# Waiting for each indirect scatter of token rows, and V rows of 160 halves: attention and mixture-of-experts layer on one core

## What is computed

```python
x = x + attention(layernorm(x))            # causal softmax attention, 16 heads
xf = layernorm(x)
shared = (silu(xf @ sg.T) * (xf @ su.T)) @ sd.T
probs = softmax(xf @ gate_w.T); topw, topi = top_k(probs, 2)
topw = topw / (topw.sum(-1, keepdims=True) + 1e-20)
routed = sum over experts e of ffn_e(xf) * (weight that token gives e, or 0)
return x + shared + routed
```

## Time and profile before

| | us |
|---|---|
| median of 3 runs | 918.35 |
| the runs | 915.56 to 918.37 |
| the profiled execution, its own time | 914.5 |
| its span in the trace | 912.8 |

### The profile page before, as it was taken

The page is one execution under the profiler, slowest core; times in us unless marked ns, Lnnn a source line. Parts: engine busy times, 40 slices in busy tenths (PEclk is TensorE's granted clock), DMA queues, the critical chain, the costliest instruction groups (busy, mean ns, idle before and its releaser), DMA issues.

```text
span 912.8 us, 25700 instructions
## 1 busy us (share of the span) xinstructions
PE 851.0 (93%) x10266; PEld 576.5 (63%) x10266; DVE 692.0 (76%) x1769; ACT 685.1 (75%) x843; POOL 714.1 (78%) x450
## 2 busy tenths in 40 slices
PE   5888999999999999999999999999999888959996
PEld 3445666666666666666666666666666564438885
DVE  6898888797979897979797979787976465434444
ACT  5466888988888889798989898888899782224442
POOL 3566898998999899899989898989889877244442
PEclk9799999999999999999999999999999999779999
DMA  6030232324242323333302020202020001112214
GB/s 185 21 110 10 56 68 65 68 56 70 63 79 61 69 74 68 71 63 79 60 5 55 5 48 1 58 2 49 2 49 2 2 2 47 42 35 69 62 44 146
DMA packets 60149, 48.33 MB, mean 53 GB/s; under 512 B 8688, under 2 KB 57714, under 8 KB 59904
## 3 DMA queue, kind: packets, MB, share of 16 engines
q1 hardware_dynamic: 57760, 42.48, 20.3%
q0 software_dynamic: 2272, 4.22, 1.3%
HBM read 13.93 MB, written 16.29 MB: 33 GB/s over the span
## 4 chain that ended last, share of the span: by engine, by line
PE 59%; DVE 24%; POOL 4%; issue 4%; DMA 3%; ACT 3%; another core or an unknown queue 2%; SPq 1%; POOLq 0%; DVEq 0%; ACTq 0%
DVE row_max L1034 10%; PE st L1312 7%; PE st L1313 7%; PE bg L1237 7%; PE pv L1344 5%; PE pv L1346 5%; PE pv L1348 4%; POOL p_parts L589 4%; DVE junk L1030 3%; PE bg L1487 3%; PE bg L1227 3%; PE bg L1204 2%; PE bg L1202 2%; PE bg L1203 2%
## 5 line engine op out<-in xcount | busy, mean ns | idle before, releaser
L589 POOL TENSOR_TENSOR p_parts<-prob,p_parts 128x1024 f16<-128x1024 f32 x320 | 612.4, 1936 | 89.9 <-ACT p_parts L724 87.9
L723 ACT ACTIVATE prob<-st,p_bias 128x1024 f32<-128x1024 f32 x320 | 331.1, 1035 | 109.8 <-PE st L1313 70.8
L724 ACT ACTIVATE p_parts<-st,p_bias 128x1024 f16<-128x1024 f32 x320 | 330.8, 1034 | 0.0
L1034 DVE TENSOR_REDUCE row_max<-bg 128x1 f32<-128x512 f32 x384 | 250.4, 684 | 6.9 <-PE bg L1237 5.4
L1344 PE MATMUL pv<-v_parts,p_parts 128*128 128x65 f16 x2176 | 233.0, 193 | 3.1 <-POOL p_parts L589 2.6
L1346 PE MATMUL pv<-v_parts,p_parts 128*128 128x64 f16 x2176 | 233.3, 195 | 0.0
L1348 PE MATMUL pv<-v_parts,p_parts 128*128 128x65 f16 x2176 | 232.2, 192 | 0.0
L1312 PE MATMUL st<-qk_parts 128*128 128x512 f16 (+3 forms) x640 | 221.2, 348 | 4.7 <-ACT p_parts L724 1.9
L1344 PEld LDWEIGHTS pv<-v_parts,p_parts 128*128 128x128 f16 x2176 | 202.5, 96 | 28.4 <-DVE attn L1086 8.8
L1313 PE MATMUL st<-qk_parts 66*128 66x512 f16 (+3 forms) x640 | 220.1, 350 | 0.0
L1237 PE MATMUL bg<-qk_parts 128*128 128x512 f16 (+3 forms) x640 | 210.7, 352 | 9.8 <-DVE row_max L1034 2.2
(11 more groups left out here) (231 smaller groups left out, 1044.9 us busy)
## 6 DMA issues: line engine op xcount, KB each, us to landing
qk_parts<-qk_parts SPq DMA_DIRECT2D x192, 64.0 KB, 2.0
row_dram<-fill SPq DMA_DIRECT2D x8, 1290.0 KB, 10.0
qk_parts<-qk_parts SPq DMA_DIRECT2D x16, 256.0 KB, 3.0
stage_raw<-ffn_w SPq DMA_DIRECT2D x16, 176.0 KB, 2.6
v_parts<-row_dram SPq DMA_DIRECT2D x39, 64.5 KB
qk_parts<-y_dram SPq DMA_DIRECT2D x8, 256.0 KB, 4.3
w_raw<-qkv_w SPq DMA_DIRECT2D x8, 192.0 KB, 2.3
down_w<-ffn_w SPq DMA_DIRECT2D x1, 1536.0 KB, 8.0
```

The source lines that it names most:

```text
L589: nc.gpsimd.tensor_tensor(o, a, b, ALU.subtract).then_inc(p_lo_ready, 1)
L723: nc.scalar.activation(o32, src, ACT.Exp, bias=p_bias[:], scale=D ** -0.5)
L724: nc.scalar.activation(o16, src, ACT.Exp, bias=p_bias[:], scale=D ** -0.5).then_inc(exp_done, 1)
L1034: nc.vector.tensor_reduce(row_max[:, t, c:c + 1], bank, AX_X, ALU.max).then_inc(bg_drained, 1)
```

## The change

Two edits. In `scatter_rows`, each indirect DMA of a half except its first now waits until `x_scattered[g]` has reached 16 for every scatter of that half issued before it. In the layout of V, a row has 160 halves in place of 129; the high part and the ones keep columns 0 to 64, and the low part moves from column 65 to column 96.

```diff
-VW = 2 * D + 1
+V_LO = 96
+VW = 160
...
                     for t in range(8 * g, 8 * g + 8):
+                        sent = 8 * r + t - 8 * g
+                        wait(pool, x_scattered[g], 16 * sent)
                         nc.gpsimd.indirect_dma_start(
...
-                    nc.vector.tensor_tensor(v_quad(i % 2, q, D + 1, VW), quad, v_quad(i % 2, q, 0, D), ALU.subtract
+                    nc.vector.tensor_tensor(v_quad(i % 2, q, V_LO, V_LO + D), quad, v_quad(i % 2, q, 0, D), ALU.subtract
...
-                    nc.tensor.matmul(out[:, 0:D], p_hi[:, n % PRING, cols], v[:, D + 1:VW],
+                    nc.tensor.matmul(out[:, 0:D], p_hi[:, n % PRING, cols], v[:, V_LO:V_LO + D],
```

## The result

| | before | after |
|---|---|---|
| median, 4 runs each, on one chip | 916.95 us | 944.11 us |
| all runs | 914.94 to 918.37 | 942.08 to 947.1 |
| the profiled execution, its own time | 914.5 | 942.08 |
| its span | 912.8 | 940.3 |

The ratio of after to before is 1.030, with a 95% interval of 1.0261 to 1.034: the changed kernel is slower by 27.2 us (24 to 31). The forecast was +24.5 us and 942.9.

What follows compares the result with a forecast made beforehand. The prediction took PE as the bound, with tile 9 made late by POOL's waiting scatters: +22.5 us delay, +2.0 clock and 0 for V's rows gave +24.5 on the 918.35 median, 942.9 us, range 932 to 951.

Steps and rivals of the forecast that it cites:

- The period: POOL's row scatters: start to landing 2.2 us plus release to start 0.8 us, 3.0 us for each waiting scatter.
- The train's end: Half 1's last row scatter on POOL starts at 845.7 us and SP goes on at 848.0.
- SP and PE behind it: SP's gather of tile 9 after the train: PE turns the tile at 850.8 instead of 828.24, +22.5 us.
- What the delay covers: Before tile 9: tile 0's 3.8 us lateness and ACT's two waits cost nothing within 24 us of PE slack.
- The result scatters: POOL's 39 result scatters queued behind the train: reached at 847.0 us, no cost.
- The clock: PE after its idle time, from 850.8 us: lower granted clock costs +2.0 us, between 0 and +4.
- V's rows: PE's V matmuls with 160-half rows: 0 us; rival that they matter in part, -8 us, 935 us, chance 0.07.
- The stretches of the earlier trace: ACT's unexplained waits near the trains, 6.48 and 9.56 us: worth nothing in the change unless one falls after 850.
- overlap: Rival: POOL prepares a scatter beneath the earlier landing; period 2.2 us, not slower, 918 us; chance 0.06.
- shorter period: Rival: POOL's scatter period about 2.4 to 2.6 us, 15 us less, 928 us; chance 0.07.
- late stall: Rival: an ACT stall falls after 850 us, +6.5 to +9.6 us, 949 to 952 us; chance 0.07.

Runs made afterwards that it cites:

- one wait a half: Ninth scatter of each half waits for the first eight, with V's rows of 160, against the kernel before: 904.58 us, ratio 0.9877.
- two in flight: Each scatter waits for the one two ahead, with V's rows of 160, against the kernel before: 899.73 us, ratio 1.0043.
- the two comparisons: V's rows of 160 halves alone, scatters unchanged, against the kernel before on two chips: 913.27 us, ratio 0.9983, and 913.51 us, ratio 0.9975.
- third group: The changed kernel, and one wait in each half with V as before, against the kernel before at 913.89 us: 945.57 and 904.36 us.
- three in flight: Each scatter waits for the one three ahead, V as before, against the kernel before at 895.12 us: 894.86 us, ratio 0.9996.

## Why the prediction was right, point by point

**The period: right in kind, 5% short.** Predicted 3.0 us, measured 3.145 and 3.17. From landing to start it was 0.78 to 0.80 (predicted 0.8) at 28 of the 30 waits and 0.85 at two, although POOL had nothing else to do but prepare. From start to landing it was 2.27 to 2.57, in the mean 2.37 (predicted 2.2): this is the mis-sized term. I had two ends of it in hand, 2.3 from SP's waits and 2.11 from a lone scatter of results, and took a value between them; the rows of the very same instruction said 2.3, and were the better ones, though still 0.07 short. Worth 15 x 0.145 + 15 x 0.17 = +4.7 us.

**The train's end.** Predicted 848.0 for SP, measured 850.97 (the chain above): +4.7 for the period, -1.8 since the train began at 752.68 and not at 754.44. That start is not a clean measure of anything: with the same V rows other traces have from 752.96 (one wait a half) to 757.11 (two in flight).

**SP and PE behind it: right.** From SP's release to the turn 853.65 - 850.97 = 2.68 us, predicted 2.74. The gather landed 1.80 us after its start, not 2.0.

**What the delay covers: right.** PE was ready for tile 9 at 853.65 - 28.61 = 825.0. Predicted was 826.6, by a slip: the text says three more tiles, the sum has 4 x 2.1; three at the named pace, 13.8 / 6 = 2.3, give 804.4 + 6.9 + 13.8 = 825.1. The slip changed nothing, since PE was idle behind either. Tile 0 at 804.97 (predicted 804.4) cost nothing. The 25.4 us can be followed through: half 1 has landed 850.96 - 812.4 = 38.6 us later, of which 10.2 by its later start (801.13 against 790.96) and the rest by its 15 waits. From that go the 8.9 us in which the landed train had waited for DVE's table, and 5.1 us of lead that the gather had: before, 828.24 - 821.28 = 6.96 us lay between its issue and the turn, now 853.65 - 851.75 = 1.90. To it come the 0.8 that SP takes from its release to the gather, which before lay within the 8.9: 38.6 - 8.9 - 5.1 + 0.8 = 25.4.

**The result scatters: right.** Six went out from 849.94 to 856.60, the first five 1.28 us apart, and PE never waited for gathered rows behind tile 9. SP did wait for result scatters, 7.2 us in seven waits ahead of its gathers from 850 on, against 11.3 in nine in before from 828 on.

**The clock: right.** Windows of after: length, busy time (count) of PE, PEld, ACT, DVE and POOL, granted clock, DMA share, GB/s, to be read as the earlier trace rows.

```profile
830.00:849.00 19.00, 0.00 (x0) 0.00 (x0) 0.00 (x0) 0.00 (x0) 6.17 (x7) 0.50 0.07 21
852.00:855.00 3.00, 1.35 (x6) 1.33 (x7) 0.29 (x1) 0.27 (x1) 2.14 (x3) 0.50 0.32 91
855.00:858.00 3.00, 3.00 (x15) 2.15 (x14) 0.50 (x2) 0.46 (x1) 1.95 (x2) 0.53 0.31 88
858.00:862.00 4.00, 4.00 (x32) 3.23 (x31) 1.91 (x6) 1.77 (x6) 0.97 (x1) 1.00 0.21 57
```

The first row is the changed kernel in one line: for 19 us no engine but POOL does anything, and POOL a third of the time. The clock is at 1.2 GHz until about 858 and at 2.4 from then on. Beyond tile 9's 25.4 us the span grew by 27.5 - 25.4 = 2.1 us; predicted 2.0. Nearly all of it lies in one step: from tile 9 to tile 10 857.69 - 853.65 = 4.04 us passed, where before had 830.36 - 828.24 = 2.12.

**V's rows: wrong, by a little.** I took 0, with -8 us as a rival. The groups of the three V matmuls by form, first with 129 halves (the kernel with the waits alone), then with 160 (after): busy us, mean ns of one, idle time before.

```profile
L1346 PE MATMUL pv<-v_parts,p_parts 128*128 128x65 f16 x2176 | 233.0, 193 | 3.1 <-POOL p_parts L589 2.6
...
L1348 PE MATMUL pv<-v_parts,p_parts 128*128 128x64 f16 x2176 | 233.3, 195 | 0.0
...
L1350 PE MATMUL pv<-v_parts,p_parts 128*128 128x65 f16 x2176 | 232.2, 192 | 0.0
```

```profile
L1347 PE MATMUL pv<-v_parts,p_parts 128*128 128x65 f16 x2176 | 230.3, 194 | 3.1 <-POOL p_parts L590 2.6
...
L1349 PE MATMUL pv<-v_parts,p_parts 128*128 128x64 f16 x2176 | 230.2, 193 | 0.0
...
L1351 PE MATMUL pv<-v_parts,p_parts 128*128 128x65 f16 x2176 | 230.2, 193 | 0.0
```

PE is busy for 698.5 us with them at 129 halves and 690.7 at 160, 7.8 us less. The eight traces with V rows of 129 halves have 231.8 to 233.5 us a line, the six with 160 have 230.2 to 231.3. Of these 7.8 us 1.4 and 2.5 reached the time in the two comparisons, and only the second excludes none. The step that failed is the comparison of two sets in the earlier trace rows: both sets are rows of 129 halves, so it could show only a cost that one has and the other does not, and 7.8 us / 544 = 0.014 us a set is barely more than the 0.01 us in which the rows are written. It was a fair argument against 23 us, and none against 8. Whether it is the pitch of 160 or the low part's place at column 96 that helps was not tried, nor why most of the gain in PE's busy time does not arrive.

**The stretches of the earlier trace rows: right in the sum, not understood.** I said that in the changed kernel they are worth nothing, gone or not, and that holds: PE has 28.6 us to spare there. But I had not seen what they are worth in the kernel before: on the third group's chip, where it takes 913.89 us, a single pause in each train wins 9.5 us. For a prediction of this change that did not matter; for a better kernel it is the larger finding.

**The rivals.** The *overlap* fell: from landing to start 0.78 us or more passed each time; so did the *shorter period*. The Trainium skill, DMA: Bandwidth & Descriptors, "Anatomy of one DMA", gives an estimate of 2.15 us for such a DMA; the trace has 2.29 and 2.56 us from start to landing in the rows above, 0.14 and 0.41 more, and 3.15 for the whole step, so here it comes near the transfer alone and is not the period. The *late stall* did not come: none of the three traces with every scatter waiting has a "remote" wait of ACT or DVE from 750 to 850 us, nor has after one of ACT up to 930. *V's rows* were worth some 2 us, not 8.

**Against which time.** I added 24.5 to the first median of before, 918.35; the runs beside those of after put it at 916.95, so that 1.4 us of my 942.9 come from the base. The change itself was 2.7 us larger than I said; in the profiled executions it was 27.5 us, 3.0 larger, of which 2.9 are the period and the earlier start together (4.7 - 1.8). In the third group it was larger still, 31.7 us.

## What stays open

- What the stall is. It was in all four traces that I read of kernels with unbroken trains on the chips where before takes 914 to 918 us (before, V's rows twice, and the waits in half 0 alone), and in no trace on the chip where it takes 895, not even with a dense train. I have no trace of the kernel before on that chip; that it runs there without stalls follows only from its time and from its relatives. Nor did three in flight run where before takes 914 to 916 us, so it is open whether waits that hold nothing back would end the stall. The 20 us between the chips are near to what the stalls add up to in a trace (6.6 + 9.6 + 2.4 = 18.6 us of ACT's waits in before), which is a match and no proof. In before a packet that fetches instructions falls 3 to 5 us ahead of each stall (at 766.3 and 798.3 us), and the stalls end about when the trains do. That a fetch waits behind POOL's DMAs would fit, but kernels without a stall have such packets in the same stretch as well, and I made no experiment that moves them.
- The changed kernel did not run on the chip where before takes 895 us. By half 1's waits (+26.7 there) and half 0's on top it should be some 50 us slower there, since there is no stall that the slack contains; this is only worked out.

## What to carry to other kernels

A wait for the landing of the DMA just ahead costs a full round trip each time (here 3.15 us in place of 1.28), because here neither the transfer nor the issuing engine's restart is hidden: count it as a latency, multiply by the number of waits, and follow what is queued behind it, here SP's gathers and PE, up to the first tile that needs the last of them. If transfers must be held back, let two or three be in flight, or wait once in the middle: on the chip without stalls, the pace with three in flight was the unbroken one, and one wait in a train of 16 cost nothing that could be measured; where the trains met stalls, two in flight and the one wait were faster than none, and three were not tried. And before pricing a change against a kernel, look whether that kernel's own unexplained waits belong to the thing being changed; what a change costs or brings can then differ from chip to chip, as here.

## What the runs showed of the hardware that I had not expected

- During trains of 16 indirect DMAs from POOL at 1.28 us each ACT stood still for up to 11.7 us at a time on some chips, and not on the one where before takes 895 us; with one pause of 2.2 us in the middle the longest waits left, of ACT or DVE, were of some 4 us.
- With two scatters in flight the spacing was 1.57 to 1.74 us, with three 1.28, the pace without waits.
- With rows of V at 160 halves and the low part at column 96 the same matmuls were busy for 690.7 us in place of 698.5.
